# A six-layer graph network on one core: GpSimd centres weights and bias rows with broadcast additions, and the written-out order of the engines' work is replaced

## The reference

```python
h = relu(layernorm(x));  x = x + L0(h, adj)   # GAT: 12 heads of 32, masked softmax over neighbours
h = relu(layernorm(x));  x = x + L1(h, adj)   # two DIR layers: bilinear scores, exp, h_lin, LayerNorm, relu
h = relu(layernorm(x));  x = x + L2(h, adj)   # two DIG layers: h h^T softmax, three value products, LayerNorm, relu
h = relu(layernorm(x));  x = x + L3(h, adj)   # GRAPHORMER: 12 heads with adj as bias, then a projection
```

## Time and profile before

| | |
|---|---|
| median of 3 runs | 2855.91 us (2854.23 to 2859.2) |
| the profiled execution's own time | 2849.21 us |
| its span, first to last instruction | 2847.5 us |
| mean granted TensorE clock | 0.987 |
| instructions | 85381 |

### The profile page before, as it was taken

How to read it: one execution, slowest core, us unless ns; L and a number is a source line. 1 busy time by engine, 2 the same in 40 slices (tenths; PEclk the granted TensorE clock), 3 DMA queues, 4 the chain that set the end, 5 groups by cost and what they waited for, 6 DMA issues and landing times. The chain is left out here.

```text
span 2847.5 us, 85381 instructions
## 1 busy us (share of the span) xinstructions
PE 2677.8 (94%) x32384; PEld 2026.1 (71%) x32384; DVE 2469.1 (87%) x6758; ACT 1950.6 (69%) x6740; POOL 1444.1 (51%) x2345
## 2 busy tenths in 40 slices
PE   5799999999999999999999999999999999999996
PEld 4567777777777777777777777777777777776764
DVE  7788898889888898889888888889898888988885
ACT  7466676676766676677676767677677667676653
POOL 4644554454544454555554544455455555555543
PEclk9899999999999999999999999999999999999998
DMA  8232333332332333233332332332332332332220
GB/s 214 78 64 55 56 65 56 55 65 57 58 61 54 55 67 56 55 66 55 57 64 56 59 61 54 56 67 56 53 67 53 57 66 54 57 66 53 56 43 20
DMA packets 546323, 175.69 MB, mean 62 GB/s; under 512 B 513665, under 2 KB 545665, under 8 KB 545665
## 3 DMA queue, kind: packets, MB, share of 16 engines
q1 hardware_dynamic: 536704, 157.64, 30.5%
q10 hardware_dynamic: 9216, 12.59, 1.3%
HBM read 31.72 MB, written 12.58 MB: 16 GB/s over the span
## 5 line engine op out<-in xcount | busy, mean ns | idle before, releaser
L981 PE MATMUL bank<-w_hi,ht 128*128 128x384 f16 x3840 | 1043.8, 327 | 0.0
L981 PE MATMUL bank<-ht,w_hi 128*128 128x128 f16 x9216 | 823.5, 221 | 21.9 <-DMA ht<-qk 16.5
L981 PE MATMUL bank<-ht,w_lo 128*128 128x128 f16 x4608 | 801.0, 221 | 0.0
L981 PEld LDWEIGHTS bank<-ht,w_hi 128*128 128x128 f16 x9216 | 724.1, 99 | 96.4 <-issue 53.2
L981 PE MATMUL bank<-w_lo,ht 128*128 128x384 f16 x1920 | 628.2, 327 | 0.0
L719 ACT ACTIVATE t<-t,few 128x128 f32<-128x128 f32 x1536 | 593.8, 391 | 7.4 <-POOL qk L605 1.6
L981 PEld LDWEIGHTS bank<-w_hi,ht 128*128 128x128 f16 x3840 | 376.6, 98 | 234.0 <-issue 15.1
L981 PEld LDWEIGHTS bank<-ht,w_lo 128*128 128x128 f16 x4608 | 454.6, 99 | 0.0
L591 POOL TENSOR_TENSOR h<-h,row 128x384 f32<-128x384 f32 x256 | 256.6, 1002 | 158.5 <-DVE h L960 158.5
L797 DVE TENSOR_TENSOR qk<-bank,qk 128x256 f16<-128x256 f32 x576 | 234.4, 418 | 106.8 <-ACT qk L710 106.3
L719 ACT ACTIVATION_READ_ACCUMULATOR t<-t,few 128x1 f32 x1536 | 292.8, 191 | 0.0
(11 more groups left out here) (122 smaller groups left out, 5428.2 us busy)
## 6 DMA issues: line engine op xcount, KB each, us to landing
x<-in_x_dram SPq DMA_DIRECT2D x64, 192.0 KB, 2.3
out_dram<-h ACTq DMA_DIRECT2D x64, 192.0 KB, 1.9
ht<-qk SPq DMA_TRANSPOSE x384, 2.8
w_hi<-in_weights_dram SPq DMA_DIRECT2D x9, 576.0 KB, 5.2
w_lo<-in_weights_dram SPq DMA_DIRECT2D x8, 576.0 KB, 5.3
adj<-in_adj_dram SPq DMA_DIRECT2D x64, 64.0 KB, 2.2
row<-in_rows_dram SPq DMA_DIRECT2D x1, 1920.0 KB, 9.6
row<-in_rows_dram SPq DMA_DIRECT2D x1, 1536.0 KB, 10.2
```

Source lines behind the costliest of these rows:

```text
L981: m = nc.tensor.matmul(out, a, b, start=(first and n == 0), stop=(last and n == 3 * len(left) - 1))
```

## The change

**The centring.** For each of the eight centred weights GpSimd issued three `tensor_scalar` additions of 128x384 (one for each of the `C` = 3 row blocks, with the mean as a per-partition scalar); it now issues one `tensor_tensor` addition of 128x1152 whose second operand is the three means, each broadcast over 384 columns. The eight `tensor_scalar` additions of the bias rows become one `tensor_tensor` of 128x3072. The semaphores count accordingly: a weight's consumer on ScalarE waits for one increment and not for three, and every user of a centred row waits for the one addition of all rows.

**The order.** `OPENING`, `BODY` and `CLOSING` of all five engines are replaced. In the opening, the set-up pieces move to the front: GpSimd's first six set-up pieces stand in a row before its seventh step of a stream, and SP issues seven pieces in a row before its first transpose. In `BODY`, SP's order is the same but for where the string is cut; on the other engines neighbours change places. TensorE's fifth becomes: `1:mix0 0:vals2 1:back0 0:gram2 3:flip5.0 4:gram4 3:flip5.1 4:vals4.0 0:aturn2 3:flip5.2 0:context2 4:vals4.1 3:scale5 3:mix5 4:aturn4 4:vals4.2 4:context4 1:proj1.0 2:vals0 1:proj1.1 1:proj1.2 3:project5 1:vals1 1:gram1 0:gram3 0:vals3.0 1:aturn1 0:vals3.1 3:load 1:context1 4:proj5.0 4:proj5.1 0:aturn3 4:proj5.2 0:vals3.2 0:context3 4:scores5 3:proj0.0 4:vals5 3:proj0.1 1:proj2.0 3:proj0.2 1:proj2.1 1:proj2.2 3:scores0 2:mix0`. So the last projection of DIR_B (`0:proj2.2`, in the next fifth's names `1:proj2.2`) now stands ahead of the neighbour's `scores 0` and of `mix 0` instead of behind `mix 0`, `vals 2` stands ahead of `back`, and `context 2`, `scale 5` and `mix 5` come ahead of `vals 4.1` or `aturn 4`.

On VectorE: `exp 5.2` moves ahead of `proj 2.0` (it stood behind `scores 0`), `proj 2.1` ahead of `turn 4`, `gram 2` ahead of `stats 1`, `soft 2` ahead of `norm 1` and `gram 4`, `turn 1` ahead of `soft 4`, `gram 3` and `vals 3.0` ahead of the `load` and `stats 0` of a new graph, `soft 3` and `norm 0` ahead of `split 0.0`, `vals 3.1` behind `turn 0` and `cnorm 1`. On ScalarE: `vals 2` moves ahead of `exp 5.1`, `gram 2` ahead of `exp 5.2`, `flip 5.0` and `aturn 2` ahead of `norm 1` and `turn 1`, `scale 5` ahead of `aturn 4`, `proj 5.1` ahead of `aturn 3` and `exp 0.2`, and `vals 5` behind `proj 0.0`, `proj 2.0` and `turn 4`. On GpSimd: `stats 1` moves ahead of `vals 2`, `context 2` ahead of `aturn 4`, `vals 0` behind `context 3` and `cnorm 3`.

```diff
@@ OPENING, BODY, CLOSING of tensor, vector, scalar, pool, sync @@
-    "pool":
-        "40401231323421w0ww010w0w011w1w020010ww21011002200001211203210211103",
+    "pool":
+        "021120wwwwww0w33ww1304412400011102001013101200220000312112012012110",
-    "sync":
-        "04w31ww2ww0w1ww3w24www0001110www2221w0w1w20www102w03",
+    "sync":
+        "2w013wwwwwww0www1w4wwwww2w0003w1110w41w2220331320w310201",
...
@@ wait_row @@
             elif r == 0 and k in range(1, 9):
-                eng.wait_ge(rows_centred, k)
+                eng.wait_ge(rows_centred, 1)
@@ gpsimd, set_up @@
                 for k, w in enumerate(CENTRED_W):
                     pool.wait_ge(w_sums, 2 * k + 2)
-                    for c in range(C):
-                        mean = means[:, 8 + k * C + c:9 + k * C + c]
-                        nc.gpsimd.tensor_scalar(stage_of(w)[:, c], stage_of(w)[:, c], mean, None, ALU.add).then_inc(w_centred, 1)
+                    mean = means[:, 8 + k * C:8 + (k + 1) * C]
+                    nc.gpsimd.tensor_tensor(stage_of(w), stage_of(w), mean.unsqueeze(2).broadcast_to((P, C, D)),
+                                            ALU.add).then_inc(w_centred, 1)
                     yield
                     if k == 0:
                         pool.wait_ge(row_sums, 2)
-                        for n in range(8):
-                            nc.gpsimd.tensor_scalar(row[:, 1 + n], row[:, 1 + n], means[:, n:n + 1], None,
-                                                    ALU.add).then_inc(rows_centred, 1)
+                        nc.gpsimd.tensor_tensor(row[:, CENTRED_ROWS], row[:, CENTRED_ROWS],
+                                                means[:, 0:8].unsqueeze(2).broadcast_to((P, 8, D)),
+                                                ALU.add).then_inc(rows_centred, 1)
                         yield
@@ scalar, set_up @@
                     if w in CENTRED_W:
-                        act.wait_ge(w_centred, C * (CENTRED_W.index(w) + 1))
+                        act.wait_ge(w_centred, CENTRED_W.index(w) + 1)
```

More of the change, by code:

```diff
@@ L129 @@
     "tensor":
-        "032311212211000330434331221312321122404414433143422323322111441040442332423432233010020044204033"
-        "434433222002101003443034043344121131100310144040044333113212114004140104400232242211421200101100"
-        "444224323220110201210011343303322",
+        "232031121221010303304343121231321122240441443343142232332121414410404232342432233301002004404203"
+        "343443232020021010343403043344412113110010314404004343131132121404014104400023224221121420010110"
+        "404242243232010120210011134330332",
     "vector":
[L134 to L137, removed]
+        "322002044032111234424121113320343434212422132233423002324142042433113100143222340030232224431404"
+        "040323033243344034113430203103044224211204333401141343330042010101434144304400140224041314214100"
+        "330322310444012202404441103121212040200410011201330102420320211441433421000123313010002214232323"
+        "101311021122312441213031431",
     "scalar":
-        "023100241134421000323143131342143112311240334404224104013421130224003211143420424240320422342230"
-        "144001033021012403224133011432220403103030143103340334120011214413212301433024412204333101421414"
-        "12042144014402311223200243234120441300233104442120320202310320012001342233431130434",
+        "034100124134420321003143313113442311121240334404224103414021123024003143211420442422400342223230"
+        "144001033021402013223413011420432203100303301140333434120011214413201312433402412203104331421141"
+        "44122014440402311223200243124230440130233142104420322020023312000101342233431130423",
     "pool":
-        "003230221134233232214114341332240344343320220402443301400404431331013004412011010042442124110023"
-        "122121103",
+        "003232201143323232214114343312204434343320220404423310040404431331010034421101010042442121140032"
+        "212121103",
     "sync":
-        "33132010344424312140003042320111410343122202140423",
+        "20103444243121400030423201114103431222021404233313",
 }
@@ L154 @@
+        "22222311302201110133330302232322112101133333223322212111133333322222333333221222333233333333",
     "vector":
[L155 to L158, removed]
@@ L159 @@
-        "33323",
+        "322004402032111234421221133140343432421223422332132231244400204134131033212423034322302044042413"
+        "433203042044033141341233000311030244212142403343043433340001034042141401341400340224042141134310"
+        "013203420041021420440321141410122420033210031101401222003203204111321132003010101222200123313131"
+        "212212021333113132122023212311201233331322121232332313212233232333322322232333323333332213332333"
+        "3333",
     "scalar":
-        "032001112443204100231331314311321131244203430444122401043114200023241311032424422422430042412323"
@@ L165 @@
+        "332111432233223222333233222222333123333333333",
     "pool":
-        "003232211343232312241143413302024434343320224004433100404044333121013004241101100202214110023212"
-        "21131233202133323122233323233313323",
+        "003232211043323232214114343322414043433232020402443300140404431330110034412101100024212110023212"
+        "21131323202113323322233323333212333",
     "sync":
-        "331320103444241321000430243210114130432221021032331321323233",
+        "20103444243121430000423210141130431222021023331321323233",
```

25 lines of the change are left out of this document (12 added, 13 removed).

## The result

The changed kernel takes 2836.17 us (median of 7 runs, 2834.76 to 2841.34) against 2855.91 us before (7 runs, 2844.90 to 2859.69): ratio 0.994, 95% interval 0.9925 to 0.9956. A second time, on another chip, it gave 0.9948 (0.9934 to 0.9963). So it is faster by 0.5 to 0.6%: 20 us here, 15 us there. The forecast was 2812 us, 44 us less than before: sign right, range right, size less than half.

What follows compares the result with a forecast made beforehand. The prediction took a ring through VectorE's queue, SP's issues and a transpose landing to set the period. Middle 38, centring 3 and opening 3 sum to 44 us: 2855.9 - 44 = 2812 us, range 2790 to 2852 (8 in 10).

Steps and rivals of the forecast that it cites:

- The ring: Middle: VectorE's queue, three SP transpose issues, a landing and back to VectorE set the period, 42.39 us in one round.
- TensorE's wait was its slack: Middle: TensorE's 1.01 us a round at `mix 0` is slack; moving `mix 0` alone would not gain.
- The stops that go, and the cover: Middle: VectorE's stops of 0.44 us (L887) and 0.39 us (L797) go, 0.61 us (L921) stays; `proj 2.2` covers `mix 0`'s wait.
- The ring becomes 42.39 - 0.44 - 0.39 = 41.56 us: Middle: removing two VectorE stops shortens the round to 41.56 us; other VectorE swaps count nothing, -0.2 to +0.3 us.
- 42.0 us, 38 us: Middle: a round of 42.0 us, 0.69 us gained, times 55 rounds gives 38 us; bounds 0 to 56 us.
- The prediction's own sign of being wrong: Middle: small `mix 0` wait, but new TensorE waits for VectorE's low halves or `ht<-qk`, the interval still 42.6 us.
- half of it: Rival: new short waits take half the middle's gain, leaving 19 + 6 = 25 us, 2831 us; chance 0.15.
- the rival that named places for the new waits: Middle: ring keeps its length, wait moves to `gram 1`, `gram 3` or `proj 5.0`; 2850 us, chance 0.17.
- Centring, 3 us: Opening: GpSimd's additions fall from 45.6 to 31.8 us; 3 us gained on the path, between 0 and 5.9.
- The opening's order, 3 us gained, -12 to +12: Opening: of 51 us of idle TensorE a tenth may return or be lost; 3 us gained, -12 to +12.
- The prediction feared SP's order: Opening: SP's first transpose stands behind seven set-up pieces, two waiting for VectorE to free a place; no row prices it.
- The end, taken as nothing: End: rearranged by a few neighbours; no gain taken, 3 us either way.

Runs made afterwards that it cites:

- e4: Kernel before with the broadcast additions and one TensorE swap, `proj 2.2` ahead of `scores 0` and `mix 0`: 2866.25 us, ratio 1.0033.
- e13: The changed kernel measured again, on another chip, against the kernel before: 2839.45 us, ratio 0.9948.
- e7: Changed kernel with TensorE's `proj 0.2` ahead of `proj 2.0`, and ScalarE's `vals 5`, `proj 0.1`, `proj 0.2` ahead of `proj 2.0` and `turn 4`: 2815.03 us, 0.9869.
- e14: Changed kernel's order with the centring of before, on the same chip as e13: 2839.80 us, ratio 0.9947 against the kernel before.
- e1: Kernel before, its order kept, with only the changed centring (broadcast additions): 2864.39 us, ratio 1.0028.
- e8: Changed kernel's order with the centring of before: 2841.84 us, ratio 0.9964 against the kernel before.
- e5: Changed kernel with one TensorE swap undone, `proj 0.2` ahead of `proj 2.0` again: 2854.26 us, ratio 1.0008 against the kernel before.
- e6: Changed kernel with ScalarE's `vals 5` and `proj 0.1` ahead of `proj 2.0` and `turn 4`: 2835.27 us, ratio 0.9939 against the kernel before.
- e9: e1 with the bias rows' one addition of 3072 columns cut into eight of 384: 2852.82 us, ratio 0.9992 against the kernel before.
- e11: First two graphs of each stream in the old order, then e7's order; row addition in eight pieces, each weight's in three: 2813.10 us, 0.9860 against before.

## Why the prediction was right in sign and wrong in size

**The ring: right, as far as shown.** The prediction said that the period is set by a ring through VectorE, and that TensorE's wait was its slack. e4 removed three quarters of that wait and got nothing, with the reserve made there.

**The stops that go, and the cover: right.** L887's stop went, L921's stayed, `mix 0`'s wait fell to 3.8 us.

**"The ring becomes 42.39 - 0.44 - 0.39 = 41.56 us": the step that failed.** That length, and the 42.0 us and 38 us from it, held only if nothing new stopped VectorE. The part-by-part account priced TensorE's move of `proj 2.2` and took nothing for VectorE's other swaps. It passed over three swaps without a price: on TensorE `proj 2.0` ahead of `proj 0.2`, on ScalarE `vals 5` and `proj 0.1` behind `proj 2.0`, on VectorE `proj 2.1` ahead of `turn 4`. It took SP's landing to stay as it was for the three transposes of the attention weights, and did not ask for `turn 2`'s.

The swaps on TensorE and ScalarE put `turn 2`'s landing, 4.4 us, into a ring of its own: VectorE, SP, landing, TensorE, ScalarE, VectorE. It stops VectorE for 1.44 us a round at `proj 2.1`, more than the 0.83 us of stops removed; other stops closed (the one ahead of `proj 2.0` fell from 0.73 to 0.12 us a round), and 0.30 us a round was left (0.36 in e13) instead of 0.69. The term "42.0 us, 38 us" was thus mis-sized: 16.5 us measured (19.8 in e13). e7, which undoes the swaps on TensorE and ScalarE alone, gives a round of 42.02 and 38.2 us of middle.

That it meets the forecast to the decimal is partly luck: it still has 0.58 us a round at `proj 2.1` and 19.3 us in all at `back`, which the forecast did not have. What VectorE's own swap cost is not shown. The prediction's own sign of being wrong did come, new waits for `ht<-qk` on TensorE (29.4 us for 10.3), with a round of 42.39 and not of 42.6. The rival "half of it", 2831 us, came nearest in number, but its 6 us from the opening and the centring were not there; the rival that named places for the new waits had `gram 1`, `gram 3` or `proj 5.0`, not `proj 2.0`.

**Centring, 3 us: wrong.** GpSimd's time was sized well (31.8 forecast, 27.1 measured), its worth not. In the new order no worth shows (e13, e14); in the old one 7 us were lost (e1). I had priced the effect on other engines only as ScalarE's waiting and not asked what a single 5 to 6 us instruction does to VectorE. After escapes the worst by its order: beside the row addition (29.07 to 34.38 us) VectorE waits 5.07 us for TensorE.

**The opening's order, 3 us gained, -12 to +12: wrong sign, in its bounds.** 7.9 us were lost by the 3000th matmul (5.7 in e13). The order alone, with the centring of before, loses as much: 8.0 us in e8 and 8.6 in e14. TensorE was busy 81.19 of the first 140 us, so 58.8 us were idle for 51. Its waits after, from 0 to 300 us:

```profile
PE bank L981 <- DMA ht<-qk: 18.4, 5, 16.1
PE bank L981 <- issue: 16.9, 8, 11.5
PE bank L1064 <- DMA t<-ht: 10.3, 2, 9.6
```

Three single waits of 16.1, 11.5 and 9.6 us, where the longest for a transpose was 6.6 us before. All three end with the landing of a transpose (the 11.5 us too, which the view puts down to "issue": its transpose is issued at 55.80 and lands 2.7 us later, and TensorE goes on at 58.62). The prediction feared SP's order. The trace does not bear that out for these three:

```profile
18.56 1.32 SPq L523 DMA_TRANSPOSE ht<-qk  x1
```

```profile
55.23 0.55 DVE L827 SCALAR_TENSOR_TENSOR qk<-h,qk 128x384 f16<-128x384 f32 x1
```

```profile
55.80 1.21 SPq L523 DMA_TRANSPOSE ht<-qk  x1
```

The first transpose is issued when it was before (18.34 us there), but lands after 6.1 us and not 2.8. Three loads of weights were still on their way then (they land at 21.1 to 24.0 us), before none. Of the 16.1 us only 3.5 are new: TensorE goes on at 24.7 us for 21.2. The one at 55.80 us is issued as soon as VectorE has done its low half. ScalarE's high half had been there since 48.09, but on VectorE four set-up operations of 1.3 to 1.4 us stood between. The three that `mix 0` waits for are issued from 74.24 us on, right behind the low half that GpSimd held until 74.21. SP's own order delayed another transpose, whose low half ended at 19.69 and which was issued at 24.86. So VectorE's set-up work, moved ahead of a `turn`, is the likelier cause of more of the loss than SP's order. No run moved either, and the cause is only argued. The end, taken as nothing, lost 0.8 us.

Sum of the profiled pair: +7.9 - 16.5 + 0.8 = -7.8 us, against -44. Of the 36 us between, the middle makes 21.5, the opening with the centring 13.9 (6 forecast, 7.9 lost), the end 0.8.

## What to carry to other kernels

Price every swap of a reordered period, on every engine's queue: one that puts a step waiting for a DMA ahead of ready work can make a new ring through that landing, and here it showed two engines on, on VectorE. Undo such a swap on all engines that share its steps, since on one alone it moves the wait (e5) or does nothing (e6).

Fewer, longer GpSimd instructions are not free because GpSimd is idle: beside a VectorE operation with two SBUF inputs their length counts. Cut them until one piece is as short as the delay that you can bear (here 384 columns, 1.2 us in the mean in e9 and 0.8 at the shortest).

The two best versions, e7's order at 2815 us and e11 at 2813 us, are 1.3 to 1.4% under the kernel before and can't be told apart.

## What the runs showed of the hardware

A two-SBUF-input operation of VectorE that takes 0.68 us took 5.79 us beside one GpSimd addition of 3072 columns, and 1.31 us beside the same addition in pieces of 384.

GpSimd's addition of a broadcast operand takes, at the shortest, 0.82 us for 384 columns (e9, L559), 2.11 us for 1152 and 5.31 us for 3072 (after): 2.1, 1.8 and 1.7 ns a column. A `tensor_scalar` of 384 columns takes 1.24 us at the shortest and 1.30 to 1.55 us in the mean (before). So the broadcast form is the cheaper one here, size for size, although it reads two tensors. The additions of 1152 columns that took up to 3.15 us began while a VectorE operation with two SBUF inputs was running (at 25.96, 41.25, 52.08 and 60.50 us in after), as the row addition of 6.42 us in e1 did.

A DMA transpose issued with three more queued behind it landed 4.3 us after its issue and reached TensorE's step after 4.4 us; the median of all `ht<-qk` transposes from 300 to 2600 us in after is 2.8 us.
